# Power of the variances ahead of the gate product, rest's low-rank product ahead of level 7, and the first routing copies and logits one step later

## The reference, cut to what matters

```python
x = x + 0.5 * moe(layernorm(x))       # 16 experts, top 2, capacity 1280
x = x + time_mix(layernorm(x))        # per head: S = w*S + k v^T, y = r (S + u k v^T)
x = x + 0.5 * moe(layernorm(x))

# moe: logits, top_k, softmax; a slot per (expert, position); a row over capacity is dropped
# end of time_mix, y in heads of 64:
mu, var = yh.mean(-1), yh.var(-1)
yn = ((yh - mu) / sqrt(var + 0.00064)) * ln_g + ln_b
return yn * g @ Wo
```

## Time and profile before

| what | value |
|---|---|
| median of 3 runs | 3041.12 us |
| the profiled execution's own time | 3043.45 us |
| its span in the profile | 3041.6 us |
| busy: PE, DVE, ACT, POOL | 2764.8, 1997.8, 1575.5, 1265.8 us |
| POOL's first and last scatter of the first routing start at | 39.51 and 227.56 us |
| SP's first load of the first experts is issued at | 236.28 us |
| SP's first load of the time mix is issued at | 1172.28 us |
| SP's first load of the second experts is issued at | 2096.83 us |

### The profile page before, as it was taken

How to read it: one execution, slowest core, us unless ns; L and a number is a source line. 1 busy time by engine, 2 the same in 40 slices (tenths; PEclk the granted TensorE clock), 3 DMA queues, 4 the chain that set the end, 5 groups by cost and what they waited for, 6 DMA issues and landing times. The chain is left out here.

```text
span 3041.6 us, 63629 instructions
## 1 busy us (share of the span) xinstructions
PE 2764.8 (91%) x21994; PEld 2212.3 (73%) x21994; DVE 1997.8 (66%) x4620; ACT 1575.5 (52%) x2733; POOL 1265.8 (42%) x1072
## 2 busy tenths in 40 slices
PE   6536999999999995899999999984999999999997
PEld 6535888888888883466666666663888888888886
DVE  5545666666666652688989898864666666566664
ACT  5424666666665652344444444432666656656663
POOL 2671322322222223457777777753222222232233
PEclk9999999999999997999999999997999999999998
DMA  9925545545544526201111111014455445445444
GB/s 343 334 94 116 91 81 89 94 77 88 95 78 86 96 33 222 98 16 44 35 53 33 54 33 55 26 38 116 82 89 95 77 86 95 79 86 94 80 70 149
DMA packets 540965, 281.28 MB, mean 92 GB/s; under 512 B 397591, under 2 KB 503131, under 8 KB 540480
## 3 DMA queue, kind: packets, MB, share of 16 engines
q1 hardware_dynamic: 478624, 202.67, 26.8%
q0 software_dynamic: 57888, 75.16, 14.6%
q10 hardware_dynamic: 4224, 0.52, 0.1%
HBM read 150.83 MB, written 146.41 MB: 98 GB/s over the span
## 5 line engine op out<-in xcount | busy, mean ns | idle before, releaser
L763 POOL DMA_INDIRECT acc_a<-ae_ob,ae_to x160 | 260.8, 1630 | 675.0 <-ACT ae_ob L712 623.0
L763 POOL DMA_INDIRECT acc_b<-be_ob,be_to x150 | 242.7, 1618 | 637.3 <-ACT be_ob L712 578.7
L730 ACT ACTIVATE be_h<-be_pH,b 128x512 f32<-128x512 f32 (+1 forms) x384 | 236.8, 617 | 359.2 <-PE be_pH L657 337.5
L730 ACT ACTIVATE ae_h<-ae_pH,b 128x512 f32<-128x512 f32 (+1 forms) x384 | 236.7, 616 | 342.1 <-PE ae_pH L657 324.1
L1478 POOL TENSOR_TENSOR m_xf<-m_tmp,m_xT 128x512 f32<-128x512 f32 x160 | 174.9, 1119 | 151.6 <-DVE m_tmp L1185 85.1
L1529 POOL DMA_INDIRECT slots_b<-m_row,m_sidx x128 | 143.1, 1118 | 109.3 <-issue 106.2
L1788 PEld LDWEIGHTS m_PP<-m_RP,m_KS 64*64 64x64 f32 x6656 | 115.6, 134 | 87.5 <-issue 86.4
L464 POOL DMA_INDIRECT slots_a<-ar_row,ar_sidx x128 | 126.0, 984 | 99.7 <-issue 73.8
L1788 PE MATMUL m_PP<-m_RP,m_KS 64*64 64x64 f32 x6656 | 130.0, 221 | 26.5 <-DVE m_A L1215 26.3
L657 PE MATMUL ae_pH<-ae_xT0h,ae_w_0h 128*128 128x512 f32 (+1 forms) x256 | 87.8, 343 | 69.3 <-DVE ae_xT0l L839 65.5
L1185 DVE SCALAR_TENSOR_TENSOR m_tmp<-m_B,m_ch,m_xx 128x512 f32<-128x512 f32 x160 | 114.0, 741 | 48.8 <-PE m_B L1895 38.5
(11 more groups left out here) (347 smaller groups left out, 9007.8 us busy)
## 6 DMA issues: line engine op xcount, KB each, us to landing
ae_stage<-in_w SPq DMA_DIRECT2D x64, 512.0 KB, 3.6
be_stage<-in_w SPq DMA_DIRECT2D x64, 512.0 KB, 3.5
slots_a<-empty SPq DMA_DIRECT2D x5, 4160.0 KB, 25.0
slots_b<-empty SPq DMA_DIRECT2D x5, 4160.0 KB, 31.6
ae_xq<-slots_a SPq DMA_DIRECT2D x252, 64.0 KB, 2.7
be_xq<-slots_b SPq DMA_DIRECT2D x252, 64.0 KB, 2.7
ar_xin<-in_x SPq DMA_DIRECT2D x16, 512.0 KB, 10.0
m_xin<-acc_a SPq DMA_DIRECT2D x16, 512.0 KB, 4.6
```

The source lines that it names most:

```text
L730: t = act.activation(dst[:, 0:SIZES[b]], pH[c % 2][:, 0:SIZES[b]], ACT.Gelu, bias=S.b1[:, bass.ds(i * (2 * FC) + (u * FC + f), 1)])
L763: pool.indirect_dma_start(S.acc[tag][:, :], bass.IndirectOffsetOnAxis(ap=to[m][:, q:q + 1], axis=0), ob[m][:, q, :], None, bounds_check=T ...
```

## The change

Four edits are made. In the routing, SP's queue holds the loads of groups 0 to 3, then the emptying 0, 1 and 2, the loads 4 and 5, the emptying 3 and 4, and the other loads. The logits of a group (PE) and the copies out of PSUM that they read (ACT) move from step g-3 to step g-2. In the time mix, POOL runs `root_spread` ahead of `gate` in the steps that have both K and L (steps 1 to 15). PE runs `low_rest` ahead of level 7 and behind the prefix of group R.

```diff
@@ route, SP
-                for g in range(XRING):
+                for g in range(4):
                     load(g)
-                    if XRING - PAIRS <= g:
-                        S.empty_rows(sp, tag, g - (XRING - PAIRS))
-                for g in range(XRING, NG):
+                for j in range(3):
+                    S.empty_rows(sp, tag, j)
+                for g in range(4, 6):
+                    load(g)
+                for j in range(3, PAIRS):
+                    S.empty_rows(sp, tag, j)
+                for g in range(6, NG):
                     load(g)
@@ route, PE
-                    if 0 <= s + 3 < NG:
-                        logits(s + 3)
+                    if 0 <= s + 2 < NG:
+                        logits(s + 2)
@@ route, ACT
                     if 0 <= s + 3 < NG:
                         normalise(s + 3)
-                        copy_turned(s + 3)
+                    if 0 <= s + 2 < NG:
+                        copy_turned(s + 2)
@@ mix_and_route, POOL
                     if live(K) and live(L):
-                        gate(K)
                         root_spread(K)
+                        gate(K)
@@ mix_and_route, PE
                     if live(R) and live(L):
                         prefix(R)
+                    if live(X):
+                        low_rest(X)
                     idle_last(L, 2)
                     if live(L):
                         level(L, 7)
-                    if live(X):
-                        low_rest(X)
```

More of the change, by code:

```diff
@@ L1567, in _ @@
                     if live(K) and live(L):
+                        root_spread(K)
                         gate(K)
-                        root_spread(K)
                     if live(Z):
```

## The result

| | median, us | runs |
|---|---|---|
| before | 3040.53 | 13 (3037.18 to 3046.01) |
| after | 3055.45 | 13 (one of 3564.0 at a mean clock of 0.755 is left out below; the others 3042.24 to 3057.69) |

The ratio is 1.0037, with a 95% interval of 1.0025 to 1.0049. The change made the kernel slower by about 11 us (by the means of the runs, with that one left out, by 12.1 us with a standard error of 1.5). The forecast was 3040.8 us, no change, with a range to 3046.

A forecast was written before the change was run, and what follows sets the result against it. It took the DMA-limited emptyings to bound the routing and DVE's `Y2` a mix step. Routing -3.0, `low_rest` 0 and time mix +2.7 made -0.3 us on the 3041.12 us median: 3040.8 us, range 3034 to 3046 for 8 in 10.

The forecast's parts named there:

- The routing: Routing: the fifth emptying passes loads 6 and 7 and lands earlier, so the scatters end earlier; -3.0 us, bounds -3.3 and 0.
- The rows of group 3: Routing rival: these rows come later than 91.9 us and the routing's gain is gone; 3043.8 us, chance 0.06.
- The power ahead of the gate product, middle steps: Time mix, steps 2 to 13: DVE's stall moves from `KS` to `dif` or just behind, without shrinking; 0 us.
- small instructions slip by: Middle-step rival: `dif` and those behind it run beside the gate product, saving 1.56 us a step; 3019 us, chance 0.12.
- the power holds DVE too: Middle-step rival: `KS` stands until the power ends, +0.8 us a step; 3050 us, chance 0.06.
- The last steps: Time mix, steps 14 and 15: little stall is saved at `mvar`, but `choose` pays 2.1 us; +0.8 and +1.7 us.
- The stall in `choose`: DVE in step 15: `choose` pays 2.1 us to the gate product while `mvar` saves only 0.4; +1.7 us.
- The start of the mix: Time mix, step 1: there is no `choose`, and `RP` meets the gate product's last 0.5 us; +0.2 us.
- `low_rest` ahead of level 7: PE, middle steps: it fills the 1.62 us wait, then PE only waits longer ahead of `turn_out`; 0 us taken, gain at most 0.05 a step.

The follow-up runs named there:

- e3_route: The changed kernel with both edits in the time mix undone, so the routing's edits alone on the kernel before; 3040.71 us, ratio 0.9989.
- those at 3087 us: Two later comparisons of several kernels in which even the unchanged kernel before took 3086.98 and 3088.39 us; the whole changed kernel took 3101.98 and 3100.83 us.
- e1_swap: The kernel before with only the power put ahead of the gate product on POOL; 3048.42 us, ratio 1.0018.
- e2_low: The kernel before with only `low_rest` moved ahead of level 7 on PE; 3048.99 us, ratio 1.0012.
- a2_after: The whole changed kernel, unaltered, timed and traced again in a later comparison with the kernel before; 3054.57 us, ratio 1.0023.
- the first comparison: The original timing of the whole changed kernel against the kernel before, 13 runs each; medians 3055.45 and 3040.53 us.

## Why the prediction was wrong

- *The routing*, -3.0: right in place and size. The trace has -3.67 and e3_route -3.4 (1.0). The rows of group 3 were in time. The forecast did not see that the gain depends on a routing bounded by the emptyings, which it is not in those at 3087 us.
- *The power ahead of the gate product, middle steps*, 0: right. `KS` went to 0.70 us, one of `dif`, `ef` and `oh` took 2.4, and e1_swap has 615.1 us for the twelve steps against 615.0. The rivals "small instructions slip by" and "the power holds DVE too" are both refuted by these rows.
- *The last steps*, +2.5: right in mechanism and nearly in size. The stretch behind the 13th store is 2.9 us longer in the profiled pair (157.45 against 154.57), 4.7 in e1_swap, and 3.4 by the means of the traces with and without the swap. The stall in `choose` cost 1.3 to 1.9 us in step 15, where 1.7 was forecast. The clock falls in that step with and without the swap.
- *The start of the mix*, +0.2: it was 2.9 us longer in the profiled pair, with a stretch at half clock that one trace of the changed kernel has and the other has not in that length. The sum had no term for such a difference between runs.
- *`low_rest` ahead of level 7*, 0: this is the step that failed. Its words were "PE only waits there longer", and the wait was rightly sized (about 1.1 forecast, 1.13 to 1.21 found), as was the one ahead of level 7 (0.6 and 0.61). But waiting longer was priced at nothing. Behind that wait the granted clock fell in four of twelve steps, at 3.2 us each, 12.9 us in all. By e2_low the move costs 4.5 (1.0) us on average without the swap. With the swap, filling this wait and that of step 15 won 5.8 (2.0) us. In the comparisons at 3087 us no such cost shows in the times.

The reasoning took the granted clock of 1.00 in the earlier trace rows as given and argued from the waits alone. There was a warning in the profile of before: its slices have a PEclk of 7 tenths where the mix starts and where it ends, and there PE waits most. The Trainium skill, "TensorE: Matmul & The Clock Gate", section "HAM oscillation — how this bites in real kernels", says that work which waits again and again between short bursts of products can lose the full clock in each of them. Its case is a kernel that waits for DMA, 3 to 5 us each time. The traces here agree that the clock can be lost again and again, and differ in the rest: PE is busy 591.64 of 615 us and the waits are of about 1 us. The section "What's actually happening" says of a kernel's start that the number of products at the lower clock differs from run to run. The runs here differ in the middle of a kernel too: a2_after's trace has no fall in the twelve steps, and that of the same kernel in the first comparison has four.

What is open: why the clock falls behind a wait of 1.13 us in some steps and not in others, why in the first comparison it fell in just every second step, whether the two edits together do more than each (6.1 + 4.5 - 3.4 = 7.2 us by their single means, 12.1 in the first comparison and 6.5 in that of a2_after), what makes up the swap's 6.1 us beyond some 3.4, and why the move of `low_rest` costs nothing in the times at 3087 us.

## What to carry to other kernels

An idle time of TensorE is not free to move, even where the sum stays the same: the products behind it may run at half the clock. Before an instruction is taken out from between a wait and what follows, look at the granted clock by short stretches, and at single runs with their mean clocks and not the median alone. One trace before and one after are not enough: here the single trace of the kernel before lacked a fall that six others with the same order have, and the difference of the pair would have been put down to the edit. Where such a wait can't be avoided, an unused product in it that is no longer than the wait is worth a trial: here one in each middle step lengthened none of them, and together with six in step 15 it brought back 5.8 (2.0) us.

## What the runs showed of the hardware

- A power on POOL (3.31 us) holds back neither a DVE product of two SBUF tiles (0.70 us) nor small instructions. A POOL product of 128 x 1024 (2.35 us) does, and it holds a DVE cast of 128 x 8 with a single input for 2.38 to 2.40 us.
- In the middle steps a fall of the clock holds for about 7 us and costs 3.2 us of a step of 51, behind a wait of only 1.1 to 1.2 us. It does not come behind every such wait, and in six traces never behind one of 1.62 us elsewhere in the step.
- A stage can change what bounds it from one comparison to the next: the same routing ended at 236.28 us with POOL never stopping, and at 271.8 us with stops of up to 9.5 us.
